# Storing the expert blocks' result rows to their tokens' places by indirect DMA, and reading them back by plain transfers

## The reference, cut to what matters

```python
router_logits = x @ gate_weight.T                       # x: (1024, 256), 8 experts
probs = softmax(router_logits)
top_v, top_i = jax.lax.top_k(probs, 2)
top_v = top_v / top_v.sum(-1, keepdims=True)
combine_w = einsum('tke,tk->te', one_hot(top_i, 8), top_v)
def expert_step(acc, inp):                              # scanned over the 8 experts
    gu, dp, w = inp                                     # gu: (1024, 256), dp: (256, 512)
    gate, up = split(x @ gu.T, 2, axis=-1)
    y = (silu(gate) * up) @ dp.T
    return acc + w[:, None] * y
```

## Time and profile before

| | us |
|---|---|
| median of 3 runs | 592.37 |
| the three runs | 592.37, 581.35, 593.75 |
| the profiled execution, whole time | 590.05 |
| its span, first to last instruction | 588.3 |
| sorting of the tokens (first scores to `row_i`) | 322.1 to 335.3 |
| stage of the 23 blocks (first gather to last result copied) | 335.6 to 509.7 |
| gathers of the result rows and `add_y` | 512.1 to 536.2 |
| fourth layer's feed-forward part, to the end | 536.2 to 588.3 |

### The profile page before, as it was taken

One profiled execution on the slowest core, in us unless ns is written; L12 is line 12 of the kernel. 1 busy time (PEld: TensorE's weight loads), 2 busy tenths in 40 slices (PEclk: granted clock), 3 DMA queues, 4 the chain that ended last, 5 costly groups with the idle time before them and its releaser, 6 DMA issues.

```text
span 588.3 us, 6654 instructions
## 1 busy us (share of the span) xinstructions
PE 412.3 (70%) x1779; PEld 265.5 (45%) x1779; DVE 408.2 (69%) x690; ACT 264.5 (45%) x638; POOL 245.9 (42%) x318
## 2 busy tenths in 40 slices
PE   0001699989798989767777259986997999610796
PEld 0001478655555655434556125643554556400364
DVE  5999847698999999997964807558466321053696
ACT  2311164767676677635785103321232233303685
POOL 4665700243966555752300223248147111164352
PEclk9999999999799999978896559998898899955899
DMA  7600000011011100000002098866887797131001
GB/s 258 245 1 0 17 3 1 2 36 37 0 37 36 36 0 18 2 0 1 2 0 73 28 370 270 279 223 232 299 292 267 247 313 245 37 90 45 1 28 45
DMA packets 19407, 60.47 MB, mean 103 GB/s; under 512 B 3024, under 2 KB 8400, under 8 KB 15792
## 3 DMA queue, kind: packets, MB, share of 16 engines
q1 hardware_dynamic: 17504, 54.99, 26.1%
q0 software_dynamic: 1872, 5.11, 3.6%
HBM read 54.98 MB, written 5.11 MB: 102 GB/s over the span
## 4 chain that ended last, share of the span: by engine, by line
DVE 38%; PE 33%; issue 12%; ACT 7%; DMA 4%; POOL 3%; DVEq 0%; ACTq 0%; SPq 0%; POOLq 0%
PE bank L1713 13%; DVE fw L899 7%; PE bank L1733 6%; DVE fw L884 6%; DVE bw L890 4%; DVE hx L1076 3%; DVE fw L895 2%; PE bank L1469 2%; DMA xb<-cond_rows,row_i 2%; POOL gy L483 2%; ACT rl L639 2%; DVE gl L1363 2%; DVE pt L1370 1%; DVE eu L873 1%; PE bank L1724 1%
## 5 line engine op out<-in xcount | busy, mean ns | idle before, releaser
L1713 PE MATMUL bank<-gu,xbT 128*128 128x512 f32 x184 | 91.4, 643 | 10.1 <-issue 9.1
L639 ACT ACTIVATE rl<-bank,cw 128x128 f32<-128x128 f32 x256 | 73.1, 379 | 43.2 <-DVE hx L1076 24.2
L1525 PE MATMUL bank<-hT,w2raw 128*128 128x512 f32 x128 | 69.4, 626 | 20.2 <-ACT hT L646 20.2
L1279 DVE TENSOR_TENSOR hm<-bank,sl 128x512 f32<-128x512 f32 x23 | 15.8, 685 | 75.0 <-PE bank L1713 40.6
L359 POOL TENSOR_TENSOR fw<-fw,bw 128x256 f32<-128x256 f32 x48 | 40.8, 850 | 56.9 <-DVE bw L890 56.9
L1713 PEld LDWEIGHTS bank<-gu,xbT 128*128 128x128 f32 x184 | 37.7, 207 | 50.4 <-issue 47.8
L1415 PE MATMUL bank<-ident,GT 128*128 128x128 f32 x64 | 11.7, 338 | 66.2 <-DVE GT L904 45.4
L899 DVE RECIPROCAL fw<-fw 128x256 f32<-128x256 f32 x32 | 55.8, 1743 | 0.6
L356 POOL TENSOR_TENSOR eu<-eu,kT 128x256 f32<-128x256 f32 x24 | 25.5, 1062 | 55.9 <-ACT eu L547 49.1
L1733 PE MATMUL bank<-dn,hT 128*128 128x256 f32 x184 | 45.1, 388 | 3.2 <-ACT hT L762 0.8
L1076 DVE SCALAR_TENSOR_TENSOR hx<-bank,rl 128x512 f32<-128x512 f32 x64 | 43.3, 678 | 5.2 <-ACT rl L639 5.1
(11 more groups left out here) (259 smaller groups left out, 901.5 us busy)
## 6 DMA issues: line engine op xcount, KB each, us to landing
gu<-in_gu SPq DMA_DIRECT2D x23, 1024.0 KB, 7.8
dn<-in_dn SPq DMA_DIRECT2D x23, 512.0 KB, 5.7
traw<-in_t SPq DMA_DIRECT2D x3, 1024.0 KB
y_rows<-yb SPq DMA_DIRECT2D x23, 128.0 KB
w1raw<-in_w SPq DMA_DIRECT2D x8, 256.0 KB, 3.2
w2raw<-in_w SPq DMA_DIRECT2D x8, 256.0 KB, 3.1
kT<-in_kt SPq DMA_DIRECT2D x4, 256.0 KB, 7.1
x<-in_x SPq DMA_DIRECT2D x2, 512.0 KB, 6.4
```

The lines of the kernel that those rows point to most:

```text
L639: ins = act.activation(rl[:, j % 2, e * P:e * P + P], bank[j][:, e * P:e * P + P], ACT.Relu, scale=cw0[:, t, bass.ds(4 * eg + e, 1)])
L1525: pe.matmul(bank[4 + o % 2][:], w2raw[:, slot, e, :], hT[:, e % 2, :], start=start, stop=stop, skip_group_check=True).then_inc(sem("y_done ...
L1713: ins = pe.matmul(bank[2 * (b % 2) + up][:], xbT[:, b % 2, k, :], gu[:, b % RING, k, up * I2:up * I2 + I2], start=(k == 0), stop=(k == KC ...
```

## The change

The order of the result rows in HBM is turned around. `y_rows` gets 2 x 1024 + 23 x 128 rows: first the rows of choice 0 in token order, then those of choice 1, then spare rows, one for each place that no token uses.

- `tile_no` counts to 15 in place of twice to 7, so that the matmul that inverts the sorting also says which choice stands at a place. Two more small DVE instructions give `row_i` (now modulo 1024) and `dest_i`, the row for each place; `slot_i` goes. POOL makes one more constant (`spare`) in an early stage.
- SP no longer stores the blocks' rows (`block_out`, 23 plain DMAs, goes). POOL stores them, in step b those of block b - 2, behind `gather_block(b + 3)` and ahead of the late sums, by an indirect DMA whose destination rows are `dest_i` (`scatter_block`, 23).
- POOL's 16 gathers at the end go. SP waits until all 23 stores have landed, and issues 8 plain loads of 256 KB each (2 for each pair of tiles) into `gy`, which is now four pairs large and lies over the weights' ring. `add_y` waits for its pair's two loads once.

The diff, cut to its core:

```diff
--- before.py
+++ after.py
@@ -150,6 +151,12 @@
         gu = sb("gu", [P, RING, KC, 2 * I2])
         dn = sb("dn", [P, RING, I2 // P, C])
         region2 = cursor[0]
+
+
+        cursor[0] = region
+        gy = sb("gy", [P, B, 2, 2, C])
+        assert cursor[0] <= region2
+        cursor[0] = region2
         sl = sb("sl", [P, 2, I2])
         hm = sb("hm", [P, 2, I2])
         hT2 = sb("hT2", [P, 2, I2 // P, P])
@@ -293,19 +299,17 @@
                 sp.dma_start(dn[:, b % RING, :, :], dn_d[bass.ds(e, 1), :, :, :].rearrange("o p k n -> p (o k) n")
                              ).then_inc(sem(f"dn_in{b % RING}"), 16)
 
-            def block_out(b):
-                sp.wait_ge(sem("y_ready"), b + 1)
-                sp.dma_start(y_d[b * P:b * P + P, :], yb[:, b % 2, :]).then_inc(sem(f"y_out{b % 2}"), 16)
-
             sp.wait_ge(sem("routed"), ROUTED["owner"])
             for b in range(NB):
                 block_weights(b)
-                if b >= RING:
-                    block_out(b - RING)
                 if b in (1, 8, 14):
                     ternary_in((1, 8, 14).index(b))
-            for b in range(NB - RING, NB):
-                block_out(b)
+            sp.wait_ge(sem("y_out0"), 16 * ((NB + 1) // 2))
+            sp.wait_ge(sem("y_out1"), 16 * (NB // 2))
+            for b in range(B):
+                for k in range(2):
+                    rows_k = y_d[k * TOK + 2 * P * b:k * TOK + 2 * P * b + 2 * P, :]
+                    sp.dma_start(gy[:, b, k, :, :], rows_k.rearrange("(t p) c -> p t c", p=P)).then_inc(sem(f"gy_in{b}"), 16)
             for t in range(NT):
                 sp.wait_ge(sem("x4_ready"), t + 1)
                 sp.dma_start(out_d[:, t, :], x[:, t, :]).then_inc(sem("out_done"), 16)
@@ -346,8 +350,8 @@
                 pool.iota(lane[:], [[1, P]], base=0, channel_multiplier=0, **kw).then_inc(sem("route_consts"), 1)
                 pool.iota(slab[:], [[1, NBW]], base=0, channel_multiplier=0, **kw).then_inc(sem("route_consts"), 1)
                 pool.iota(edge[:], [[P, E2]], base=0, channel_multiplier=0, **kw).then_inc(sem("route_consts"), 1)
-                pool.iota(tile_no[:].rearrange("p (k t) -> p k t", k=2), [[0, 2], [1, NT]], base=0,
-                          channel_multiplier=0, **kw).then_inc(sem("route_consts"), 1)
+                pool.iota(tile_no[:], [[1, 2 * NT]], base=0, channel_multiplier=0, **kw).then_inc(sem("route_consts"), 1)
+                pool.iota(spare[:], [[P, NBW]], base=2 * TOK + 1, channel_multiplier=1, **kw).then_inc(sem("route_consts"), 1)
                 pool.iota(lane1[:], [[0, 1]], base=1, channel_multiplier=1, **kw).then_inc(sem("route_consts"), 1)
 
             def wkv_sums(n, blk, p):
@@ -442,6 +446,12 @@
                                         bass.IndirectOffsetOnAxis(ap=row_i[:, b:b + 1], axis=0)
                                         ).then_inc(sem(f"xb_in{b % RING}"), 16)
 
+            def scatter_block(b):
+
+                pool.wait_ge(sem("y_ready"), b + 1)
+                pool.indirect_dma_start(y_d, bass.IndirectOffsetOnAxis(ap=dest_i[:, b:b + 1], axis=0), yb[:, b % 2, :], None
+                                        ).then_inc(sem(f"y_out{b % 2}"), 16)
+
             def late_value(i):
                 n = 3 * NBLK + i
                 wait(pool, sem("euv_ready"), n)
@@ -467,6 +477,10 @@
             for b in range(NB):
                 if b + RING < NB:
                     gather_block(b + RING)
+                if b == 2:
+                    pool.wait_ge(sem("routed"), ROUTED["dest"])
+                if b >= 2:
+                    scatter_block(b - 2)
                 if b < 2 * NBLK:
                     late_sum(b // 2, 1 - b % 2, ("den", "num")[b % 2])
                     if b % 2 and b // 2 + 1 < NBLK:
@@ -477,20 +491,8 @@
                     ternary_write((6, 12, 18).index(b))
 
 
-            def gather_y(t, k):
-                i = 2 * t + k
-                wait(pool, sem("y_added"), i - RING + 1)
-                pool.indirect_dma_start(gy[:, i % RING, :], None, y_d,
-                                        bass.IndirectOffsetOnAxis(ap=slot_i[:, k, t:t + 1], axis=0)
-                                        ).then_inc(sem(f"xb_in{i % RING}"), 16)
-
-            pool.wait_ge(sem("routed"), ROUTED["slot"])
-            pool.wait_ge(sem("y_out0"), 16 * ((NB + 1) // 2))
-            pool.wait_ge(sem("y_out1"), 16 * (NB // 2))
-            for t in range(NT):
-                for k in range(2):
-                    gather_y(t, k)
-
+            scatter_block(NB - 2)
+            scatter_block(NB - 1)
 
             def rms_stats(mean_sq, root, absmax, out, sum_name, max_name, n, out_name):
                 pool.wait_ge(sem(sum_name), n)
@@ -1234,8 +1236,12 @@
             chain(dve.tensor_scalar(row_f[:, 0, :], bank[7][:, 0:NBW], -1.0, None, ALU.add))
             chain(dve.scalar_tensor_tensor(out=row_f[:, 1, :], in0=bank[7][:, NBW:2 * NBW], scalar=float(P), in1=row_f[:, 0, :],
                                            op0=ALU.mult, op1=ALU.add))
-            dve.tensor_scalar(row_i[:], row_f[:, 1, :], 0.0, None, ALU.max).then_inc(sem("routed"), 1)
-            dve.tensor_copy(slot_i[:], slots[:, 0, :, :]).then_inc(sem("routed"), 1)
+            chain(dve.tensor_scalar(row_f[:, 2, :], row_f[:, 1, :], float(TOK), -float(TOK), ALU.is_ge, ALU.mult))
+            dve.scalar_tensor_tensor(out=row_i[:], in0=row_f[:, 1, :], scalar=0.0, in1=row_f[:, 2, :],
+                                     op0=ALU.max, op1=ALU.add).then_inc(sem("routed"), 1)
+            chain(dve.scalar_tensor_tensor(out=row_f[:, 3, :], in0=row_f[:, 1, :], scalar=0.0, in1=spare[:],
+                                           op0=ALU.is_lt, op1=ALU.mult))
+            dve.tensor_tensor(dest_i[:], row_f[:, 1, :], row_f[:, 3, :], ALU.add).then_inc(sem("routed"), 1)
 
             def softmax():
                 dve.wait_ge(sem("lexp_ready"), 1)
@@ -1313,11 +1319,11 @@
             def add_y(t):
 
                 for k in range(2):
-                    i = 2 * t + k
-                    dve.wait_ge(sem(f"xb_in{i % RING}"), 16 * (len(range(i % RING, NB, RING)) + i // RING + 1))
                     if k:
-                        dve.wait_ge(sem("y_added"), i)
-                    ins = dve.scalar_tensor_tensor(out=x[:, t, :], in0=gy[:, i % RING, :], scalar=cw2p[:, k, t:t + 1], in1=x[:, t, :],
+                        dve.wait_ge(sem("y_added"), 2 * t + 1)
+                    else:
+                        dve.wait_ge(sem(f"gy_in{t // 2}"), 32)
+                    ins = dve.scalar_tensor_tensor(out=x[:, t, :], in0=gy[:, t // 2, k, t % 2, :], scalar=cw2p[:, k, t:t + 1], in1=x[:, t, :],
                                                    op0=ALU.mult, op1=ALU.add)
                     ins.then_inc(sem("y_added"), 1)
 
@@ -1817,7 +1823,7 @@
         args.append(nc.dram_tensor("in_" + name, a.shape, mybir.dt.from_np(a.dtype), kind="ExternalInput").ap())
     out = nc.dram_tensor("out_x", (P, NT, C), F32, kind="ExternalOutput").ap()
     cond_rows = nc.dram_tensor("cond_rows", (TOK, C), F32, kind="Internal").ap()
-    y_rows = nc.dram_tensor("y_rows", (NB * P, C), F32, kind="Internal").ap()
+    y_rows = nc.dram_tensor("y_rows", (2 * TOK + NB * P, C), F32, kind="Internal").ap()
     build(nc, *args, cond_rows, y_rows, out)
     got = run_bass_kernel_spmd(nc, [arrays], core_ids=[0]).results[0]["out_x"]
     return np.ascontiguousarray(got.transpose(1, 0, 2)).reshape(xs.shape)
```

More of the change, by code:

```diff
@@ L45 @@
 ROUTED_SCALE = 2.5
-ROUTED = {"mk": 1, "lsub": 2, "owner": 3, "rows": 4, "slot": 5}
+ROUTED = {"mk": 1, "lsub": 2, "owner": 3, "rows": 4, "dest": 5}
 SUMMED = {"logit": 1, "place": 2, "rows": 3}
@@ L124, in build @@
         lane1 = sb("lane1", [P, 1])
+        spare = sb("spare", [P, NBW])
         region = cursor[0]
@@ L174, in build @@
         yb = sb("yb", [P, 2, C])
-        gy = sb("gy", [P, RING, C])
         rtraw = sb("rtraw", [P, KC, E2])
@@ L183, in build @@
         owner_i = sb("owner_i", [P, NBW], I32)
-        row_f = sb("row_f", [P, 2, NBW])
+        row_f = sb("row_f", [P, 4, NBW])
         row_i = sb("row_i", [P, NBW], I32)
-        slot_i = sb("slot_i", [P, 2, NT], I32)
+        dest_i = sb("dest_i", [P, NBW], I32)
         cw2p = sb("cw2p", [P, 2, NT])
@@ L1181, in per_token @@
                 return r2[:, i, :, 0:1].to_broadcast([P, NT, E2])
-            dve.wait_ge(sem("route_consts"), 10)
+            dve.wait_ge(sem("route_consts"), 11)
             dve.wait_ge(sem("summed"), SUMMED["logit"])
@@ L1678, in _ @@
             logits(3).then_inc(sem("summed"), 1)
-            pe.wait_ge(sem("route_consts"), 10)
+            pe.wait_ge(sem("route_consts"), 11)
             pe.wait_ge(sem("routed"), ROUTED["mk"])
```

## The result

| | before | after |
|---|---|---|
| median of 5 runs each on one chip, us | 589.12 | 592.25 |
| the profiled execution, us | 590.05 | 596.73 |
| its span, us | 588.3 | 595.0 |
| its mean granted TensorE clock | 0.907 | 0.911 |

What follows compares the result with a forecast made beforehand. POOL's place in its program, not PE, was taken to hold up PE twice in the block stage, and 16 gathers the end. On 590.05 us, +0.2 + 9.9 - 8.9 = +1.2 gave 591.3, range 580 to 602.

Steps and rivals of the forecast that it cites:

- Steps 13 to 22: Last part of the block stage: POOL need only be in time for gathers and result buffers; cost 0.
- code change: Unexplained POOL idle time around each of three all-reduces, taken as loading other code: 8.19, 11.0 and 9.42 us before the next arithmetic.
- The landing: Time from a scatter's start on POOL until its rows have landed, taken as 3.1 us from block 8's gather.
- The rival of the two-deep buffer: Scatters take 1.65 us of POOL and land in 8.59, so yb holds ACT at blocks 5 and 11: about 600 us; chance 0.25.
- The scatters ahead of the write-outs: Steps 4 to 12 on POOL: nine scatters at 1.2 us delay the write-outs by 3.6, then 9.9 us; stage +9.9.
- The new wait on ACT: ACT's copy of block b waits for scatter b - 2; PE loses 3.8 and 3.3 us, hidden behind late weights.
- The end: From last copy into yb to last add_y: 8 plain loads replace 16 gathers, pairs 2.1 us apart; -8.9 us.
- the prediction's own signs of being wrong: Write-outs not moving, gate_up(9) waiting on anything but its weights, or load pairs over 3 us apart.
- The sorting: One more chained DVE instruction ahead of row_i, before the first gather: +0.2 us.
- The stores off SP: 23 plain DMA issues leave SP's queue; they had covered nothing, so cost 0.
- that the store is covered: Rival: scatters hide in POOL's idle time and gaps, so only the end counts: 581.3 us; chance 0.18.
- code change of their own: Rival: each of 16 scatters between arithmetic brings two POOL idle times of 8 us: over 700 us; chance 0.02.

Runs made afterwards that it cites:

- the stage alone: Kernel before with POOL scatters in place of SP's block stores, to the same ordered rows, and the 16 end gathers kept: 602.46 us, ratio 1.0233.

## Why the prediction was wrong, step by step

- **The step that failed** is "Steps 13 to 22: POOL must only be in time for the gathers and the result buffers ... Cost 0". It measured +3.77 in the profiled execution. I had checked the gather behind the third code change, and not the result buffer: the copy of block 19 needs scatter 17 landed, which stands behind that same code change. The kernel with four buffers shows it. How much of it a median execution pays isn't shown: the same wait cost PE 0.66 and 0.77 us in two other kernels, and the median with four buffers is only 1.6 us lower. The argument was at hand, since I had made it for scatters 3 and 9, and the weights gave cover only there.
- **The landing** was taken as 3.1 us from one gather beside a nearly empty queue. In this kernel it took 4.0 (scatter 2, 383.50 to 387.47), 2.5 (scatter 3) and 2.9 us (scatter 4), but 6.1 (scatter 5, 409.59 to 415.67), 7.8 (scatter 8, 430.46 to 438.30, and scatter 11, 456.52 to 464.35) and 9.55 us (scatter 17) beside the weights. The median over the 23 scatters is 6.0 us, about twice what was taken. Traffic alone doesn't order them: scatter 3 landed while the DMA engines moved 101 GB/s and scatter 5 at 390, but scatter 2 took 4.0 us at 289 and scatter 17 took 9.55 at 242. What makes a landing long stays open. The rival of the two-deep buffer had the right mechanism and size, 8.59, and the wrong places: it put them at blocks 5 and 11, where the waits stayed hidden, and gave 600. That 592.25 still lies near the stated 591.3 owes something to luck: in the profiled pair the cost put at 0 (3.77) and the two stretches sized too small (0.9 and 0.8) make 5.4 us more than the sum, and the medians lie only 3.1 us apart.
- **The scatters ahead of the write-outs.** By scatters and sorting `gate_up(9)` was to move by 3.8 us and moved by 6.56; `gate_up(15)` by 10.1 and moved by 10.97. The price of a scatter was 1.3 us, not 1.2. The code changes weren't constant: behind the first all-reduce +2.33, ahead of the second -2.3 (8.40 to 6.06), behind it -1.3 (11.02 to 9.67). Together they give back 1.3 us. The second write-out still came 11.2 us later (441.95 to 453.13) for 9.9 forecast, and without that luck it would have been 12.5. The kernel with eight more gathers confirms the mechanism, write-out to `traw` to weights.
- **The new wait on ACT**: the copy of block 5 came 11.0 us later, for 9 forecast. PE was ready for block 9 7.4 us later (404.52 to 411.89), for 3.8. Half of the 3.6 us more is that `block_down(6)` started at 402.06, 1.8 us behind the 400.3 of the forecast, and half that it ran at the lower clock after the waits (3.64 us, for 1.96 at full clock). It stayed hidden, with 4.42 us to spare for 5.0, only since the weights were later too; four buffers didn't start `gate_up(9)` earlier.
- **The end**: -8.12 for -8.9. The first addition came 6.1 us behind the last copy, for 6.5, but the pairs 3.4 us apart, for 2.1, at 200 GB/s for the 372 of the busiest stretch. From the first addition to the fourth sigmoid it took 12.3 us, for 11.1 forecast. That the pairs came over 3 us apart was one of the prediction's own signs of being wrong, and it came true.
- **The sorting**: +0.2 forecast. It can't be read from this pair: the first gather starts 0.9 us later (336.50 for 335.59), the first stretches already lay 0.5 us apart at 134 us, and by the first all-reduce of the stage (380.96 in both) nothing of it is left.
- **The stores off SP**: 0, and nothing in the kernels with the all-reduces speaks against it. In the kernel before without all-reduces a store does stand ahead of `traw`, and its going is worth 1.2 us.
- **The level.** The sum said +1.2 on one profiled execution of 590.05, which put the stated 591.3 beneath the shown median of 592.37, although the sum was a small loss. So the text forecast a time just below the shown median while its own sum spoke for one above it. Measured: +3.1 in the medians (589.12 to 592.25), 1.0% by the ratio, +6.7 in the profiled executions.
- **The rivals**: that the store is covered falls (the write-outs moved, in the kernel after, in the stage alone and with eight more gathers), and scatters bring no code change of their own (late sums follow them by 0.03 us).

## What to carry to other kernels

A store that moves onto a queue with long stops takes the stops into its landing: list for every buffer which store frees it, at each stop and not only at the first, and take the landing from a stretch with the same traffic. When a helper engine is late in several ways at once, moving one of the waits only exposes the next; look for what makes the engine late. Here three tiny reductions over partitions on POOL were worth more than the whole change, and once they were gone the same change turned from a loss of up to 1% into a gain of 1.3%.

## What the runs showed of the hardware

The idle time ahead of an all-reduce on POOL and ahead of the next arithmetic instruction isn't a constant. In a stretch without weight traffic (1 to 2 GB/s from 126 to 142 us) it was 5.56 and 6.88 us (before, at 134.32 and 141.57), 5.73 and 6.81 in the kernel after. Beside the weights it was 6.06 to 10.03 ahead of the all-reduce and 7.13 to 11.02 behind it. Behind the first all-reduce of the stage it was 8.19 and 8.49 in the two kernels without added indirect DMAs, and 10.44 to 11.02 in the five with them. Why is open: the weights' transfers and the extra transfers both differ in that stretch, and no run separates them. The Trainium skill (GPSIMD Engine Reference, 2.1 Instruction dispatch) gives approximately 6 us for the first call of freshly loaded code. If the idle times are such loads, which no run here shows, the quiet stretch agrees, beside traffic these runs show up to 11, and the return to ordinary arithmetic costs as much again.

Two scatters took POOL 1.83 and 2.02 us, at 430.46 and 480.80 in the kernel after, in place of 0.96 to 1.01. DVE rounded a matrix of 128x2048 from 430.88 to 432.17 and from 480.68 to 481.97, and neither scatter ended before DVE had (432.29 and 482.82). The same holds for the gather at 381.55, which ended at 383.20 with the rounding done at 383.07.
